# One index copy for a whole ring of gathers, in a graph network of four layers on one NeuronCore

## The chip, the cores and the metric

The kernel runs on one core of a Trainium2 chip. Its engines are TensorE (PE, matrix products), VectorE (DVE), ScalarE (ACT), GpSimd (POOL) and SyncE (SP); each works through its own list of instructions, and they meet only at semaphores. Sixteen DMA engines move data between the device memory and the on-chip memory. The metric is device microseconds of one execution; the time given is the median of several runs. A difference is spoken of as a share of that time.

## What is computed

Four graph layers over 6,250 nodes with 256 features and 100,000 edges, sorted by their target node. Each layer normalises the rows, works on the edges and adds its result to `x`:

```
x = x + L0(h)   # attention: leaky(xl[src] + xr[dst]) -> logits -> softmax over the edges of a node -> weighted sum of xl[src]; then an FFN and two batch norms
x = x + L1(h)   # w = alpha[rel]; sums of w * support[col] at row, and of w * support[row] at col
x = x + L2(h)   # two convolutions: agg[dst] += x[src]; agg @ W_msg + x @ W_self
x = x + L3(h)   # attention with 8 heads: s_u[src] + s_v[dst] -> softmax -> weighted sum of x[src]
```

For this case only one step matters: all four layers need the rows `table[src[e]]` of every edge `e`. That is a gather of 100,352 rows (784 tiles of 128 edges, the last one padded) of 1 KB, and it is made five times: once in L0, once in L1, twice in L2, once in L3.

## The kernel before

**Edges and tiles.** The edge list is cut into `ET = 784` tiles of 128 edges. The source node of each edge lies on chip as a column of integers: `gidx` is 128 x 784, column `t` holding the 128 sources of tile `t`. One indirect DMA, issued by GpSimd, reads one such column and fetches 128 table rows, one to a partition.

**Groups and rings.** The tiles are fetched in groups of `per` tiles. In L0 a group is 4 tiles and the ring of row buffers holds 8 groups; in the three plain passes (L1, L2 twice) it is 4 tiles and 6 groups; in L3 it is 8 tiles and 6 groups. So a pass has 196 groups, or 98 in L3.

**What sets the order.** `gather` (L1001 to L1015) is all that GpSimd does in these passes. For each group it waits until its ring slot is free (L1008, L1009), calls `index_columns` (L996), and issues its indirect DMAs (L1012). `index_columns` copies the group's 4 or 8 index columns out of `gidx`, at an offset that a register holds, to the fixed place `idx[:, b, :]` of slot `b` (L998), waits for that copy on the semaphore `s_own_p` (L999), takes the semaphore back (L1000), and returns the columns. The indirect DMA takes its indices from there. `turns` (L55 to L76) writes the loop: here its body is one turn of the ring, so slot numbers are constants in the code.

**Who frees a slot, who uses it.** SyncE runs `landed_groups` (L965 to L994) beside it. It waits until a group's rows have landed and counts it (`s_landed`, L976, L979), and half a ring later, when the visits that use a group are over, gives its slot back (`ring_free`, L987). In L0 it also writes each group's rows to `edge_rows` in device memory (L1248); in L3 its own loop does that (L1880, L1886 to L1889) and frees the slot when the writes are done and VectorE has read the scores. TensorE multiplies one-hot matrices with the rows (L1103 in the plain passes; L1292, L1304 and L1317 for one visit of L0), and VectorE adds the products to the sums (L956), makes the one-hots (L941) or the features of L0 (L1369, L1376).

**What comes between.** Dense products, softmax passes and a scatter pass lie between the gathers. In the scatter pass (L1722) GpSimd also issues indirect DMAs, each behind a wait and a register operation of its own, without any copy of indices.

Of the kernel before, what the change touches and what calls it, by code (L numbers as in the profile page):

```python
# [5 lines left out]
I32 = mybir.dt.int32  # L6
# [4 lines left out]
P = 128  # L11
# [4 lines left out]
ET = 784  # L16
# [9 lines left out]
GS = 2 * VG  # L26
EG = 4
NEG = ET // EG
RG, RG0 = (6, 8)
# [33 lines left out]
def turns(eng, total, body, lag, steady=None):  # L63
    first = -(-lag // body) * body
    loops = max(0, ((steady or total) - first) // body)
    if loops < 2:
        first, loops = total + lag, 0
    for v in range(first):
        yield Turn(v, v, total, False)
    if loops:  # L70
        with eng.Fori(0, loops) as i:
            for k in range(body):
                yield Turn(i * body + (first + k), first + k, total, True)
        for v in range(first + loops * body, total + lag):
            yield Turn(v, v, total, False)

def build(nc, t, out):
    with ExitStack() as top:
        made = {}

        def own(name):
            made[name] = made.get(name, 0) + 1
            return name if made[name] == 1 else f'{name}_{made[name]}'

        def sb(name, shape, dt=F32, ctx=top):
            return ctx.enter_context(nc.sbuf_tensor(own(name), shape, dt))
# [4 lines left out]
        def sem(name):  # L91
            return top.enter_context(nc.semaphore(name))
# [18 lines left out]
        gidx = sb('gidx', [P, ET], I32)  # L111
# [32 lines left out]
        own_v, own_a, own_p = (sem(f's_own_{k}') for k in 'vap')  # L144
# [801 lines left out]
        def rows_count(name, n=2):  # L946
            return [Count(sem(f's_rows_{name}{b}')) for b in range(n)]
# [45 lines left out]
                sp.wait_ge(ring_free[b], 1)  # L993
                sp.sem_inc(ring_free[b], -1)  # L994

        def index_columns(g, u, ring, per, idx):  # L996
            b = u.c % ring
            g.tensor_copy(idx[:, b, :], gidx[:, bass.ds(u.val * per, per)]).then_inc(own_p, 1)  # L998
            g.wait_ge(own_p, 1)  # L999
            g.sem_inc(own_p, -1)  # L1000
            return [idx[:, b, j:j + 1] for j in range(per)]  # L1001

        def gather(g, table, rows_of, s_rows, ring, per, free, idx):
            top_row = g.to_reg(NP - 1)

            def fetch(u):
                b = u.c % ring
                g.wait_ge(free[b], 1)  # L1008
                g.sem_inc(free[b], -1)  # L1009
                rows = index_columns(g, u, ring, per, idx)  # L1010
                for j in range(per):
                    g.indirect_dma_start(out=rows_of(b * per + j), out_offset=None, in_=table, in_offset=bass.IndirectOffsetOnAxis(ap=rows[j], axis=0), bounds_check=top_row, oob_is_err=True).then_inc(s_rows[b].sem, 16)  # L1012
            for t_ in turns(g, ET // per, ring, 0):
                fetch(t_.at(0))

        def plain_pass(name, table, acc, acc_flat, width, weighted, fold=None, own=None):
            NB = 4
            s_rows = rows_count(name, RG)
            with ExitStack() as ctx:
                G = sb('rows_in', [P, RG * EG, width], F32, ctx)  # L1020
                idx = sb('gather_rows', [P, RG, EG], I32, ctx)
                hot = sb('hot', [P, 2, GS, P], F32, ctx)
                wgt = sb('step_weights', [P, S], F32, ctx) if weighted else None
                ps = [bank(f'ps_p{i}', ctx) for i in range(NB)]
# [196 lines left out]
        def attention_fetch0(LG, attc, room):  # L1221
# [3 lines left out]
            s_rows = rows_count('att0_', RG0)  # L1225
# [2 lines left out]
            row_free = [sem(f's_row_free{b}') for b in (0, 1)]  # L1228
            with ExitStack() as ctx:
                feat = sb('feat', [P, 2, 2 * D], F32, ctx)  # L1230
                idx = sb('gather_rows', [P, RG0, EG], I32, ctx)
                featT = sb('featT', [P, 2, 4, P], F32, ctx)
                psX = [bank(f'psX{b}', ctx) for b in (0, 1)]
                psF = [bank(f'psF{b}', ctx) for b in (0, 1)]
# [620 lines left out]
        def attention_fetch3(LG, SV, rows_room, T_room):  # L1855
            R3 = 6
# [5 lines left out]
            s_rows = rows_count('att3_', R3)  # L1862
# [4 lines left out]
            read3 = [sem(f's_slot_read3{b}') for b in range(R3)]  # L1867
            with ExitStack() as ctx:
                psS = [bank(f'psS{b}', ctx) for b in (0, 1)]
                idx = sb('gather_rows', [P, R3, GS], I32, ctx)  # L1870
                with phase() as block:

                    @block.sync
# [492 lines left out]
```

## Time and profile before

| | |
|---|---|
| Median of 3 runs | 10797.18 us (10796.2 to 10806.08) |
| The profiled execution, its own time | 10752.12 us |
| Its span, first to last instruction | 10750.4 us |
| TensorE busy, mean granted clock | 6331.9 us (59%), 0.739 |
| TensorE weight loads | 4941.0 us (46%) |
| GpSimd busy | 5855.2 us (54%) |
| VectorE busy | 5005.6 us (47%) |
| ScalarE busy | 1331.9 us (12%) |
| DMA, mean over the span | 126 GB/s |

The page cuts the span in 40 slices of 269 us and gives each engine's busy share in tenths. GpSimd's row is `3777740000288888777775777747777167763000`: it has work only in the gathers and the scatter pass, and there it stands at 7 or 8. A busy 7 isn't a free 3: what lies between two instructions of GpSimd has to be looked up in the order of time, and whether it is waiting for someone in the list of waits. The kernel's clock figure is the share of full speed (2.4 GHz) at which TensorE was allowed to run.

### The profile page before, as it was taken

The numbers are of one execution on the slowest core, as the hardware profiler recorded it, in microseconds if no ns is written. First come the engines' busy times: TensorE is split into PE (matmuls) and PEld (weight loads), VectorE is DVE, ScalarE is ACT, GpSimd is POOL, SyncE is SP. The second block draws the span as 40 slices with busy tenths as digits, with TensorE's granted clock in tenths as the row PEclk, the third lists the DMA queues.
The fourth block names the chain that finished last, engine by engine and source line by source line (L and its number), as shares of the span: only waits on it lengthen the run. The fifth ranks groups of instructions, "written<-read, shape, count | busy, mean of one in ns | idle before, by whom it ended". The sixth has DMA issues, their size and how long they took to land. (4 is left out here: it accounts for less than half of the span.)

```text
span 10750.4 us, 137753 instructions
## 1 busy us (share of the span) xinstructions
PE 6331.9 (59%) x24674; PEld 4941.0 (46%) x24675; DVE 5005.6 (47%) x12212; ACT 1331.9 (12%) x3940; POOL 5855.2 (54%) x5805
## 2 busy tenths in 40 slices
PE   4888875757466666555554555555555642222575
PEld 2888864546344444433333444444444442222454
DVE  6555558885444444355553222242222321114888
ACT  2222211213222222100001000010000300000000
POOL 3777740000288888777775777747777167763000
PEclk9898878988777777676766777677777655555798
DMA  4666674541377777644433222222222166663454
GB/s 147 189 190 187 186 231 152 169 136 35 69 104 105 104 104 105 111 134 137 133 117 91 82 82 82 82 75 81 83 83 83 41 193 204 201 193 99 129 170 155
DMA packets 835068, 1358.92 MB, mean 126 GB/s; under 512 B 112279, under 2 KB 488661, under 8 KB 834981
## 3 DMA queue, kind: packets, MB, share of 16 engines
q0 software_dynamic: 315328, 634.04, 26.7%
q1 hardware_dynamic: 385684, 562.46, 16.0%
q10 hardware_dynamic: 133968, 161.50, 4.8%
q8 instruction: 26, 0.43, 0.0%
q14 instruction: 62, 0.50, 0.0%
HBM read 943.05 MB, written 414.50 MB: 126 GB/s over the span
## 5 line engine op out<-in xcount | busy, mean ns | idle before, releaser
L1012 POOL DMA_INDIRECT rows_in<-table,gather_rows x2352 | 2500.5, 1063 | 1034.2 <-issue 511.1
L1103 PE MATMUL ps_p<-rows_in,hot 128*128 x5280 | 2000.5, 542 | 1584.6 <-SPq L976 1328.8
L1103 PEld LDWEIGHTS ps_p<-rows_in,hot 128*128 128x128 f32 x5280 | 1360.3, 271 | 2180.1 <-issue 1928.7
L1722 POOL DMA_INDIRECT scatter_sums<-regionC,idx x880 | 1387.3, 1576 | 307.1 <-issue 246.0
L956 DVE TENSOR_TENSOR regionC<-regionC,ps_p 128x257 f32 (+2 forms) x1320 | 558.6, 423 | 1767.9 <-DVEq L953 1569.1
L1464 PE MATMUL ps_p<-regionA 128*128 128x265 f32 (+1 forms) x3520 | 969.4, 435 | 426.0 <-DVE regionC L956 194.4
L1464 PEld LDWEIGHTS ps_p<-regionA 128*128 128x128 f32 x3520 | 735.3, 214 | 659.8 <-DVE regionC L956 239.3
L1012 POOL DMA_INDIRECT regionB<-table,gather_rows x784 | 848.4, 1082 | 344.5 <-issue 272.2
L1012 POOL DMA_INDIRECT regionC<-table,gather_rows x784 | 817.1, 1042 | 296.7 <-issue 265.1
L1927 PE MATMUL psS<-dst_scores,regionA 128*128 x1760 | 393.4, 362 | 793.7 <-issue 385.4
L1927 PEld LDWEIGHTS psS<-dst_scores,regionA 128*128 128x128 f32 x1760 | 383.7, 330 | 803.4 <-issue 803.4
L1795 PE MATMUL psC<-regionC 128*128 128x128 f32 x1760 | 370.5, 377 | 649.1 <-PEq L1793 647.8
L1807 PE MATMUL psO<-regionA,regionC 128*128 x1760 | 675.1, 552 | 8.8 <-PEq L1806 1.8
L1795 PEld LDWEIGHTS psC<-regionC 128*128 128x128 f32 x1760 | 319.2, 272 | 753.3 <-issue 752.9
L956 DVE TENSOR_TENSOR regionB<-regionB,ps_p 128x265 f32 (+1 forms) x880 | 372.5, 423 | 586.1 <-DVEq L953 472.5
L1537 POOL MEMSET ones<- 128x128 f32 x2 | 0.4, 206 | 1109.1 <-POOLq L2052 940.3
L1807 PEld LDWEIGHTS psO<-regionA,regionC 128*128 128x128 f32 x1760 | 495.1, 295 | 120.7 <-issue 23.8
L1496 DVE TENSOR_TENSOR regionA<-regionA,logits 128x512 f32<-128x512 f32 x880 | 547.6, 684 | 0.0
L1317 PEld LDWEIGHTS psL<-att_cols,featT 128*128 128x128 f32 x3520 | 526.0, 215 | 37.6 <-issue 4.9
L1292 PE MATMUL psX<-regionA,regionB 128*128 x1760 | 528.7, 429 | 21.7 <-PEq L1288 18.6
L1369 DVE TENSOR_TENSOR feat<-regionB,psX 128x512 f32<-128x512 f32 x440 | 301.8, 686 | 499.5 <-DVEq L1368 375.0
L998 POOL COPY gather_rows<-gidx 128x4 int32 (+1 forms) x882 | 221.4, 251 | 468.1 <-POOLq L1009 461.8
(303 smaller groups left out, 8011.7 us busy)
## 6 DMA issues: line engine op xcount, KB each, us to landing
regionA<-edge_rows SPq DMA_DIRECT2D x880, 256.0 KB, 3.2
edge_rows<-regionB SPq DMA_DIRECT2D x196, 512.0 KB
edge_rows<-regionC SPq DMA_DIRECT2D x392, 256.0 KB
regionC<-srcrow_d SPq DMA_DIRECT2D x220, 256.0 KB
scatter_sums<-zero_rows ACTq DMA_DIRECT2D x8, 6400.0 KB, 42.3
regionA<-scatter_sums ACTq DMA_DIRECT2D x49, 1024.0 KB
rows_in<-table,gather_rows POOLq DMA_INDIRECT x2352
regionB<-rrow_d ACTq DMA_DIRECT2D x110, 256.0 KB
```

The lines of the kernel that those rows point to most:

```text
L956: v.tensor_tensor(dst_, dst_, ps[(u.c * VG + j) % nbank][:, 0:width], ALU.add).then_inc(s_add.sem, 1)
L1012: g.indirect_dma_start(out=rows_of(b * per + j), out_offset=None, in_=table, in_offset=bass.IndirectOffsetOnAxis(ap=rows[j], axis=0), boun ...
L1103: x = te.matmul(ps[(u.c * VG + j) % NB][:, 0:width], hot[:, b, 2 * j + k, :], at_tile(G, slot[j] * 2 + k), start=k == 0, stop=k == 1)
L1292: x = te.matmul(psX[b][:, k * D:(k + 1) * D], spread[:, ub, at:at + P], at_tile(A256, nt), start=True, stop=True)
L1317: x = te.matmul(psL[gb][:, col:col + HEADS0], featT[:, b, 2 * k + c, :], attc[:, c, :], start=c == 0, stop=c == 1)
L1369: v.tensor_tensor(feat[:, b, :], G[:, bass.ds(slot * 2, 2), :].rearrange('p a c -> p (a c)'), psX[b][:, :], ALU.add).then_inc(own_v, 1)
L1464: x = te.matmul(ps[(u.c * VG + j) % NB][:, 0:width], hot[:, b, 2 * j + k, :], Gs[:, b * GS + 2 * j + k, :], start=k == 0, stop=k == 1)
L1496: v.tensor_tensor(o, i, w, ALU.mult).then_inc(aux_full[b], 1)
L1722: g.indirect_dma_start(out=scat, out_offset=bass.IndirectOffsetOnAxis(ap=idx[:, b, j:j + 1], axis=0), in_=sums[:, b, j, :], in_offset=None ...
L1795: x = te.matmul(psC[b][:, j * P:(j + 1) * P], hot[:, b * Q + j, :], same[:, b * Q + j, :], start=True, stop=True)
L1807: x = te.matmul(psO[2 * b + j // 2][:, j % 2 * D:(j % 2 + 1) * D], pairs[:, b * Q + j, :], at_tile(SUP, nt[j // 2]), start=True, stop=True)
L1927: x = te.matmul(psS[b][:, j * HEADS3:(j + 1) * HEADS3], spread[:, b, j * P:(j + 1) * P], at_tile(SV, nt[j // 2]), start=True, stop=True)
```

## The change

Before, GpSimd copies the indices of one group at a time, 4 or 8 columns, with a wait for the copy in each group. After, it copies the indices of a whole turn of the ring at once (24, 32 or 48 columns), to one of two buffers in turn, at the head of each turn, and ahead of the wait for the ring's first slot. The DMAs take their index columns from that buffer. The loop's body is two turns of the ring instead of one, so that the buffer's number is a constant in the code. `idx` is twice as large. Nothing else changes.

```
-        def index_columns(g, u, ring, per, idx):
-            b = u.c % ring
-            g.tensor_copy(idx[:, b, :], gidx[:, bass.ds(u.val * per, per)]).then_inc(own_p, 1)
-            g.wait_ge(own_p, 1)
-            g.sem_inc(own_p, -1)
-            return [idx[:, b, j:j + 1] for j in range(per)]
-
         def gather(g, table, rows_of, s_rows, ring, per, free, idx):
             top_row = g.to_reg(NP - 1)
+            groups = ET // per
+
+            def indices(u):
+                n = ring if not isinstance(u.val, int) else min(ring, groups - u.val)
+                g.tensor_copy(idx[:, u.c // ring % 2, 0:n * per], gidx[:, bass.ds(u.val * per, n * per)]).then_inc(own_p, 1)
+                g.wait_ge(own_p, 1)
+                g.sem_inc(own_p, -1)
 
             def fetch(u):
                 b = u.c % ring
+                if b == 0:
+                    indices(u)
                 g.wait_ge(free[b], 1)
                 g.sem_inc(free[b], -1)
-                rows = index_columns(g, u, ring, per, idx)
                 for j in range(per):
-                    g.indirect_dma_start(out=rows_of(b * per + j), out_offset=None, in_=table, in_offset=bass.IndirectOffsetOnAxis(ap=rows[j], axis=0), bounds_check=top_row, oob_is_err=True).then_inc(s_rows[b].sem, 16)
-            for t_ in turns(g, ET // per, ring, 0):
+                    at = b * per + j
+                    g.indirect_dma_start(out=rows_of(at), out_offset=None, in_=table, in_offset=bass.IndirectOffsetOnAxis(ap=idx[:, u.c // ring % 2, at:at + 1], axis=0), bounds_check=top_row, oob_is_err=True).then_inc(s_rows[b].sem, 16)
+            for t_ in turns(g, groups, 2 * ring, 0):
                 fetch(t_.at(0))
...
-                idx = sb('gather_rows', [P, RG, EG], I32, ctx)
+                idx = sb('gather_rows', [P, 2, RG * EG], I32, ctx)
```

The two other allocations of `idx`, in L0 and L3, change in the same way.

GpSimd's list at the head of the gather loop of L0, before. `gather_rows` is `idx`, `regionB` holds the ring of row buffers:

```order
L998 ISA [waits s_ring_free0]
L998 COPY gather_rows<-gidx 128x4
L1012 DMA regionB<-table,gather_rows 128x256 [waits s_own_p]
L1012 DMA regionB<-table,gather_rows 128x256 x3
L998 ISA [waits s_ring_free1]
L998 COPY gather_rows<-gidx 128x4
L1012 DMA regionB<-table,gather_rows 128x256 [waits s_own_p]
L1012 DMA regionB<-table,gather_rows 128x256 x3
```

The same place, after:

```order
L71 ISA
L1002 COPY gather_rows<-gidx 128x32
L1014 DMA regionB<-table,gather_rows 128x256 [waits s_own_p,s_ring_free0]
L1014 DMA regionB<-table,gather_rows 128x256 x3
L1014 DMA regionB<-table,gather_rows 128x256 [waits s_ring_free1]
L1014 DMA regionB<-table,gather_rows 128x256 x3
```

The wait for the slot has moved from the copy to the group's first DMA, and the copy and its own wait are gone from every group but the first of a turn.

The head of the gather loop of L3, after; its ring slots are freed by `s_slot_free30` to `s_slot_free35`, and `regionC` holds its rows:

```order
L1002 COPY gather_rows<-gidx 128x48
L1014 DMA regionC<-table,gather_rows 128x264 [waits s_own_p,s_slot_free30]
L1014 DMA regionC<-table,gather_rows 128x264 x7
L1014 DMA regionC<-table,gather_rows 128x264 [waits s_slot_free31]
L1014 DMA regionC<-table,gather_rows 128x264 x7
```

Here 48 DMAs follow one copy, where one copy stood ahead of each 8.

## Rows read from the trace of the kernel before

**Rows 1.** Busy time by stage: the five gathers, all engines.

```profile
core 0: us, PE busy (x) PEld busy (x) DVE busy (x) ACT busy (x) POOL busy (x), PEclk, DMA share, GB/s
260.50:1510.50 1250.00, 1116.77 (x6995) 1029.50 (x6996) 676.12 (x1094) 259.63 (x437) 904.26 (x980) 0.88 0.61 187
4530.50:5719.50 1189.00, 676.21 (x1752) 463.28 (x1752) 626.38 (x1416) 0.00 (x0) 842.68 (x980) 0.69 0.43 130
5782.40:7029.40 1247.00, 736.56 (x2046) 518.00 (x2046) 343.68 (x598) 38.64 (x97) 900.86 (x980) 0.72 0.28 82
7142.50:8388.90 1246.40, 729.99 (x2046) 520.03 (x2046) 341.84 (x598) 38.62 (x97) 900.85 (x980) 0.73 0.28 82
8611.90:9792.40 1180.50, 392.19 (x1755) 382.51 (x1756) 207.57 (x733) 0.00 (x0) 838.13 (x882) 0.50 0.68 200
```

**Rows 2.** Waits of GpSimd in the third gather, then in the fifth: total, times, longest.

```profile
POOL gather_rows L998 <- POOLq L1009: 63.0, 1, 63.0
...
POOL gather_rows L998 <- POOLq L1009: 266.9, 9, 223.1
```

**Rows 3.** GpSimd in order of time, third gather: start, length, instruction, idle before it.

```profile
6302.58 1.01 POOL L1012 DMA_INDIRECT rows_in<-table,gather_rows  x1 [0.30 <-issue]
6303.90 1.01 POOL L1012 DMA_INDIRECT rows_in<-table,gather_rows  x1 [0.30 <-issue]
6304.91 0.20 POOL L998 COPY gather_rows<-gidx 128x4 int32 x1
6305.90 1.04 POOL L1012 DMA_INDIRECT rows_in<-table,gather_rows  x1 [0.79 <-POOLq L1000]
...
6310.91 0.19 POOL L998 COPY gather_rows<-gidx 128x4 int32 x1
6311.89 1.67 POOL L1012 DMA_INDIRECT rows_in<-table,gather_rows  x1 [0.79 <-POOL gather_rows L998]
```

**Rows 4.** GpSimd in order of time, scatter pass.

```profile
3211.29 1.56 POOL L1722 DMA_INDIRECT scatter_sums<-regionC,idx  x1 [0.30 <-issue]
3213.16 1.56 POOL L1722 DMA_INDIRECT scatter_sums<-regionC,idx  x1 [0.30 <-POOLq L1716]
```

**Rows 5.** Line L998, all copies: duration in ns, least, median, most.

```profile
L998 POOL COPY gather_rows<-gidx x882: 185/193/1268, 260.6 to 9780.9; 128x4 int32 x153, 128x8 int32 x19, 128x4 int32<-128x4 int32 x4, 128x8 int32<-128x8 int32 x1
```

**Rows 6.** Copies of L998 alone by stage: length, GpSimd busy (count), clock, DMA.

```profile
260.50:1510.50 1250.00, 56.00 (x196) 0.88 0.61 187
4530.50:5719.50 1189.00, 40.60 (x196) 0.69 0.43 130
5782.40:7029.40 1247.00, 50.69 (x196) 0.72 0.28 82
7142.50:8388.90 1246.40, 52.94 (x196) 0.73 0.28 82
8611.90:9792.40 1180.50, 21.14 (x98) 0.50 0.68 200
```

**Rows 7.** VectorE in order of time, beside the last row of Rows 3.

```profile
6311.43 1.22 DVE L941 TENSOR_TENSOR hot<-iota,rel 128x1024 f32<-128x1024 f32 x1
```

**Rows 8.** A wide GpSimd instruction, from the groups of instructions.

```profile
L257 POOL IOTA regionA<- 128x392 f32 x1 | 0.5, 453 | 0.0
```

**Rows 9.** TensorE in order of time, first gather: starts of four visits' transposes.

```profile
1001.27 0.75 PE L1304 MATMUL psF<-ident,feat 128*128 128x128 f32 x4 [1.85 <-PEq L1302]
...
1005.51 1.09 PE L1304 MATMUL psF<-ident,feat 128*128 128x128 f32 x4
...
1009.09 0.63 PE L1304 MATMUL psF<-ident,feat 128*128 128x128 f32 x4
...
1011.24 0.64 PE L1304 MATMUL psF<-ident,feat 128*128 128x128 f32 x4
```

**Rows 10.** GpSimd in order of time, a longer pause of the third gather.

```profile
6269.72 1.01 POOL L1012 DMA_INDIRECT rows_in<-table,gather_rows  x1 [1.76 <-issue]
```

**Rows 11.** DMA queues during the third gather, the code's own queue.

```profile
q14 instruction: 3, 0.02, 0.0%
```

More of the change, by code:

```diff
@@ L1230, in attention_fetch0 @@
                 feat = sb('feat', [P, 2, 2 * D], F32, ctx)
-                idx = sb('gather_rows', [P, RG0, EG], I32, ctx)
+                idx = sb('gather_rows', [P, 2, RG0 * EG], I32, ctx)
                 featT = sb('featT', [P, 2, 4, P], F32, ctx)
@@ L1869, in attention_fetch3 @@
                 psS = [bank(f'psS{b}', ctx) for b in (0, 1)]
-                idx = sb('gather_rows', [P, R3, GS], I32, ctx)
+                idx = sb('gather_rows', [P, 2, R3 * GS], I32, ctx)
                 with phase() as block:
```

## The prediction, made before the changed kernel was run

> **What bounds the kernel now.** The page's busy shares name no engine: TensorE 59%, GpSimd 54%, VectorE 47%. So I read the kernel by stage, taking the five stretches from a gather's first index copy to its last DMA [rows 1]. They add up to 6112.9 us of the span of 10750.4. GpSimd is busy for 71 to 72% of each. TensorE is at 54 to 59% in the three plain passes, at 33% in the fifth stretch, and at 89% in the first. VectorE is between 18 and 54%. No engine is full, so I looked at whom GpSimd waits for. In the third gather its only wait for a ring slot is the one ahead of the first group (63.0 us, once) [rows 2]; the first, second and fourth gathers show the same, one wait at the start. From then on a slot was always free: the consumers are ahead, and GpSimd never stops. Only the fifth gather has more, nine waits with 266.9 us, 223.1 of them ahead of the first group; some 44 us in eight waits lie inside it [rows 2].
>
> What GpSimd does in that time stands in its own order of time [rows 3]. Within a group, one indirect DMA follows the other at 1.32 us (6302.58, 6303.90): 1.01 us of work and 0.30 us of idle. Where a group ends, the index copy starts at once (6304.91 = 6303.90 + 1.01) and takes 0.20 us, but the next DMA starts only 0.79 us after its end. From one group's first DMA to the next one's is 5.99 us (6305.90 to 6311.89). Four DMAs at 1.32 would be 5.28. The copy therefore costs 0.71 us of a period of 5.99, of which its own busy time is only 0.2: the rest is the wait for its semaphore. This is what bounds the five gathers: GpSimd's chain of issue, copy included.
>
> **What the change removes.** Copies before: 196 in each of four gathers and 98 in the fifth, 882 in all [rows 5, 6]. After, one to a turn of the ring: 196/8 gives 25 in the first, 196/6 gives 33 in each plain pass, 98/6 gives 17 in the fifth, so 25 + 99 + 17 = 141. Removed: 171 in the first gather, 163 in each plain pass, 81 in the fifth, 741 together. At 0.71 us each: 121 + 3 x 116 + 57 = 526 us.
>
> **What is left at a group's boundary.** The wait for the slot and the taking back of its semaphore stay, and now stand directly ahead of a DMA instead of ahead of a copy. Does the gap there fall to the 0.30 us that lies between DMAs, or stay at 0.79? Two places speak to it. The copy starts with no gap after the fourth DMA [rows 3], although the slot's wait, its semaphore and a register operation stand between them: they ran while the DMA did. And in the scatter pass each DMA has a wait and a register operation of its own, some of them two waits, and the gap is still 0.30 us, also where the trace names the semaphore line L1716 as what ended it [rows 4]. So I take 0.30. The other end is 0.79, by which a removed copy brings only its own 0.2 us: 741 x 0.2 = 148 us.
>
> **What is added.** The 141 copies left are wider, 24 to 48 columns instead of 4 or 8. No row shows that width. The nearest are a copy of 4 columns at 0.193 us [rows 5] and a generated tile of 392 columns at 0.453 us [rows 8]. By the first the width costs nothing, by the second 0.26 us each, 37 us in all. Since 48 columns are nearer to 4 than to 392, I take 0.05 each: 7 us. The first copy of each gather now runs ahead of the wait for the first slot, which is 63.0 us long in the third gather [rows 2], so that one is hidden: 5 x 1 us at most, left in the bounds. The loops turn half as often, 68 times instead of 136; their branch is hidden in the zero gap ahead of a copy [rows 3], and it still stands ahead of one.
>
> **What contention does.** The copies' mean is more than 0.193 us: 56.00/196 = 0.29 in the first gather, 0.21 in the second, 0.26 and 0.27 in the next two, 0.22 in the fifth [rows 6]. With these means a removed copy is worth 0.78, 0.70, 0.75, 0.76 and 0.71 us, and the sum is 549 us. But the order of time shows what the excess is [rows 3, 7]: the DMA that starts at 6311.89 takes 1.67 us, 0.66 more than its neighbours, while VectorE's one-hot instruction of 1.22 us had begun at 6311.43 and ended at 6312.65. GpSimd's next instruction stands still until VectorE's is over, whichever it is. The number of such VectorE instructions doesn't change, so most of the delay moves from the copies to DMAs. Of the 23 us between the two sums I keep 10.
>
> The Trainium skill states this as a lock ("SBUF — State Buffer", section "Who interferes with whom"): a VectorE instruction with two inputs in SBUF blocks a GpSimd instruction that reads SBUF until it has finished, and the one that issued second waits. The rows just read agree in kind [rows 3, 7]. The same section infers that descriptor generation isn't touched by such a VectorE instruction; here an indirect DMA was, and the row decides. By that inference the delay would have belonged to the copies alone, and the sum would be the 549 us.
>
> **The fifth gather** won't give all of its 57 us. Of its waits for slots inside the stretch, some 44 us, a part is set by others: the rows must land, be written out again and be read. With GpSimd sooner at the slot, each such wait grows by what it gained since the last one. Eight waits in 98 groups leave most of the gain; I take off 12 us (the ends: 0, and all 57). What it competes for is the DMA engines, 0.68 busy at 200 GB/s [rows 1].
>
> **Sum.** 526 - 7 + 10 - 12 = 517 us. The profiled execution took 10752.12 us, so 10235 for the changed kernel on the same terms; the span hides nothing, as launch and end are within 2 us of it. The runs' median is 45 us above the profiled execution, 10797.18, and what is asked for is a median: 10797 - 517 = 10280 us, 4.8% less.
>
> **Rivals.**
>
> *A, the boundary gap stays.* The 0.79 us isn't the copy's but belongs to a group's start, and only 0.2 us a copy goes: 10797 - 148 = 10649. For it: the first DMA of a group is 1.04 us long against 1.01 [rows 3], so something does differ there. Against it: the scatter pass [rows 4]. Chance 0.06.
>
> *B, TensorE becomes the bound of the first gather.* There it is busy for 1116.77 of 1250 us [rows 1]. If that work couldn't shrink, then with the same slack of 7% for its pauses the stage would stop at 1200 us: 50 instead of 121 us gained, and if the fifth gather gives nothing either, another 45 lost: 10280 + 71 + 45 = 10396; with the first alone 10351. Against it: one visit takes 4.24 us in one place (1001.27 to 1005.51) and 2.15 us in another (1009.09 to 1011.24) [rows 9], and the stage's granted clock is 0.88, a mean of stretches at full clock (2.4 GHz) and at half. 441 visits at 2.15 us are 948 us; the gather would take 1250 - 121 = 1129. The pace asked of TensorE goes from 2.83 to 2.56 us a visit, which it keeps at 2.4 GHz and not at 1.2. The half-speed stretches are short beside a ring of 8 groups, 42 us of work, which evens them out. Chance 0.10.
>
> *C, the end on the other side: loading code.* The loop body of a gather is twice as long, 96 DMAs in the fifth gather instead of 48, with waits beside them. If the branch back no longer found its target at hand, each of the 68 turns would wait for code. The price of a turn is unknown; the longest pause ahead of a DMA that no one is named for is 1.76 us, 1.46 over the usual [rows 10], which would give 68 x 1.46 = 99 us, so 10379. It decides the sign from 517/68 = 7.6 us a turn, and at 10 us a turn the kernel would be at 10797 - 517 + 680 = 10960. Against it: the code's queue moved 3 packets in the whole third gather [rows 11], with the loops of all engines running, so loops of the present sizes load nothing. Chance 0.03 for the small price and 0.02 for one that makes the kernel slower.
>
> The Trainium skill has the rule behind this ("Runtime: NRT & Kernel Launch", section "Instruction fetch mechanics"): a taken branch whose target isn't in the two pages held forces a fetch, and a page is 256 instructions. By it the longest new body, some 130 instructions by the list, still stays inside, and rival C would cost nothing. No row here shows a loop that leaves the window.
>
> **How the numbers follow.** The forecast has 0.79, A 0.06, B 0.10, C 0.05. The forecast's own bounds: all of the copies' excess gone, no wider copies, the fifth gather in full, the five first copies hidden, gives 549 + 5 = 554, so 10243; runs differ by some 10 us and the median may sit 0.3% off the profile's offset, so 10210 at the low end. At the high end, 37 us for wide copies, no credit for contention and nothing from the fifth gather: 526 - 37 - 57 = 432, so 10365. To take in most of B and the small price of C the range goes to 10400: 10210 to 10400 leaves out A, the dear C and the edges, less than 2 in 10. Faster by more than 0.2% (22 us, about what a measurement of this kernel can tell from no change): everything but the dear C and an unforeseen nothing, 0.96. Within 0.2%: 0.02. Slower: 0.02.
>
> **What the new profile would show.** Copies: 141 instead of 882. In GpSimd's order of time, the gap between the last DMA of a group and the first of the next is 0.30 us; 0.79 us there means A. The five stretches: about 1130, 1075, 1130, 1130 and 1135 us. GpSimd's busy share in them rises to some 76%, since idle goes rather than work. Waits for ring slots inside the first four gathers stay near nothing; if the first shows many, it is B. Pauses of over 1 us at every turn of the loop mean C. If GpSimd's gaps close as told and the stretches still don't shrink, the reading that GpSimd sets their length is wrong, and with it the whole forecast.

## The result, and the profile after

The changed kernel took 10956.85 us (median of 4 runs, 10934.54 to 10962.57), beside 10799.43 us for the kernel before: the ratio is 1.0141, with a 95% interval of 1.0124 to 1.0159. It is slower; the forecast was 10280. The profiled execution took 10954.17 us, against 10752.12.

First what the profile after says of GpSimd. The copies of the new line, then the third gather at a turn of the ring, in order of time (start, length, instruction, idle before it):

```profile
L1002 POOL COPY gather_rows<-gidx x141: 202/214/1254, 255.3 to 9955.2; 128x24 int32 x96, 128x32 int32 x24, 128x48 int32 x16, 128x16 int32<-128x16 int32 x5
```

```profile
6575.67 1.01 POOL L1014 DMA_INDIRECT rows_in<-table,gather_rows  x1 [0.30 <-issue]
6576.69 0.21 POOL L1002 COPY gather_rows<-gidx 128x24 int32 x1
6577.79 1.05 POOL L1014 DMA_INDIRECT rows_in<-table,gather_rows  x1 [0.89 <-issue]
6579.14 1.01 POOL L1014 DMA_INDIRECT rows_in<-table,gather_rows  x1 [0.30 <-POOLq L1011]
```

There are 141 copies, as worked out, each 0.02 us longer than a narrow one (214 ns against 193 in [rows 5]). The thirteen DMAs ahead of this copy, over the ends of three groups, all follow each other at 0.30 us where no group finds its slot taken: GpSimd's part went as told. But the stages, which answer to [rows 1], did not all follow:

```profile
255.30:1706.10 1450.80, 1179.11 (x6760) 1066.73 (x6761) 657.77 (x1062) 250.21 (x422) 839.94 (x809) 0.80 0.51 160
4740.70:5975.80 1235.10, 614.80 (x1752) 433.75 (x1752) 637.04 (x1413) 0.00 (x0) 807.40 (x817) 0.67 0.42 125
6035.50:7211.20 1175.70, 670.44 (x2032) 476.62 (x2033) 336.50 (x590) 38.91 (x98) 855.75 (x817) 0.71 0.30 88
7321.50:8497.60 1176.10, 663.16 (x2034) 474.44 (x2034) 335.68 (x590) 38.84 (x98) 847.15 (x817) 0.69 0.30 88
8722.00:9977.20 1255.20, 382.52 (x1712) 373.02 (x1712) 204.24 (x712) 0.00 (x0) 812.98 (x801) 0.50 0.63 187
```

The first gather went from 1250 to 1451 us, the second from 1189 to 1235, the fifth from 1180 to 1255; the two of layer 2 fell from 1247 to 1176. Together that is +180 us; the other 22 of the 202 lie between the stages. What lengthens them stands in the waits of the first gather, kernel after, then before (who waited, for whom, total us, times, longest):

```profile
ACT featT L1275 <- ACTq L1274: 998.5, 326, 20.6
DVE feat L1371 <- DVEq L1370: 522.0, 239, 21.0
POOL regionB L1014 <- POOLq L1011: 373.6, 101, 10.4
```

```profile
ACT featT L1273 <- ACTq L1272: 689.9, 307, 5.3
DVE feat L1369 <- DVEq L1368: 345.3, 222, 3.6
```

GpSimd, which had waited for no slot here, now does: 373.6 us in 101 gaps put down to line L1011, the wait for the slot. In 12 of them only the usual 0.30 or 0.89 us passed; the other 89 hold 366 us. ScalarE's longest wait for TensorE's transposes grew from 5.3 to 20.6 us. The start of the gather shows how. First TensorE and ScalarE, then GpSimd, all in the kernel after (start, length, instruction, idle before it):

```profile
276.53 0.63 PE L1306 MATMUL psF<-ident,feat 128*128 128x128 f32 x4
279.01 0.63 PE L1306 MATMUL psF<-ident,feat 128*128 128x128 f32 x4
284.18 0.60 ACT L1275 ACTIVATE featT<-psF 128x512 f32<-128x512 f32 x1 [9.24 <-ACTq L1274]
288.21 1.08 PE L1306 MATMUL psF<-ident,feat 128*128 128x128 f32 x4 [1.88 <-issue]
302.66 0.60 ACT L1275 ACTIVATE featT<-psF 128x512 f32<-128x512 f32 x1 [17.88 <-ACTq L1274]
303.40 1.84 PE L1319 MATMUL psL<-att_cols,featT 128*128 128x4 f32 x8 [12.39 <-PEq L1312]
```

```profile
301.62 1.01 POOL L1014 DMA_INDIRECT regionB<-table,gather_rows  x1 [0.30 <-issue]
302.94 1.01 POOL L1014 DMA_INDIRECT regionB<-table,gather_rows  x1 [0.30 <-issue]
303.95 0.22 POOL L1002 COPY gather_rows<-gidx 128x32 int32 x1
305.06 1.04 POOL L1014 DMA_INDIRECT regionB<-table,gather_rows  x1 [0.89 <-issue]
```

TensorE writes the transposes of one visit and the next to two buffers in turn, each with a semaphore of its own, and can't begin those of the visit after next before ScalarE has copied the first. So a copy belongs to the last transposes of its own buffer: the one at 284.18 to those of 276.53, the one at 302.66 to those of 279.01. These were over at 279.64, and ScalarE, which in between made one copy and issued one DMA, began their copy 23.0 us later. TensorE's next products stood for 12.39 us behind that. From 279 to 303 GpSimd issued a DMA every 1.32 us. The transposes of 288.21 were copied at 323.8.

I measured the lateness of all 440 copies of the first gather: from the end of the copy's own transposes, or of ScalarE's copy before where that is later, to the copy's start. It is 0.13 us where nothing holds it. Over 3 us late were 5 in the kernel before (3.8 us at most) and 67 in the kernel after (20.6 at most); over 5 us none and 34.

Is it TensorE's signal that is late, or the engine that waits for it? The trace also keeps the times at which each semaphore changed, though not all of them where copies are late. For the copy at 302.66 the semaphore was raised at 302.54, not at 279.64. Where both changes of a copy's semaphore are on record, the raising came over 1 us after the end of TensorE's transposes in 131 of 332 cases (34.4 us at most) in the kernel after, and in 65 of 271 (2.8 at most) in the kernel before. Where it is on record, the semaphores that ScalarE and VectorE raise for TensorE in the same gather were never raised over 0.2 us after the end of the instruction, in either kernel. So it is TensorE's signals that come late. They do so while GpSimd's indirect DMAs run: between the first gather and the next indirect DMAs, 1376 us, the kernel after has all 787 such waits for TensorE on record, none with a late signal. No other engine's DMAs are needed for it: in its third gather GpSimd's queue moves all but 0.06 of the 101.58 MB, and at least 93 of 373 such signals on record are over 1 us late.

### The profile page after: what moved, and what is told of

It reads as the page before. It is cut to its first block and busy times, and to the rows that moved or that the text cites. A ratio compares the mean times of both kernels' runs of the same rounds, so it can differ in the third digit from the quotient of the medians.

```text
span 10952.4 us, 135271 instructions
## 1 busy us (share of the span) xinstructions
PE 6223.2 (57%) x24674; PEld 4885.9 (45%) x24675; DVE 5015.1 (46%) x12212; ACT 1331.5 (12%) x3940; POOL 5628.6 (51%) x5064
## 5 line engine op out<-in xcount | busy, mean ns | idle before, releaser
L1105 PE MATMUL ps_p<-rows_in,hot 128*128 x5280 | 1831.2, 506 | 1654.4 <-issue 527.8
L1105 PEld LDWEIGHTS ps_p<-rows_in,hot 128*128 128x128 f32 x5280 | 1269.1, 253 | 2176.6 <-issue 1965.2
L1319 PEld LDWEIGHTS psL<-att_cols,featT 128*128 128x128 f32 x3520 | 557.6, 228 | 218.8 <-issue 185.5
L1319 PE MATMUL psL<-att_cols,featT 128*128 128x4 f32 x3520 | 509.8, 268 | 155.3 <-ACT featT L1275 67.4
L1294 PE MATMUL psX<-regionA,regionB 128*128 x1760 | 562.5, 451 | 19.7 <-PEq L1290 17.9
```

Source lines behind the costliest of these rows:

```text
L1105: x = te.matmul(ps[(u.c * VG + j) % NB][:, 0:width], hot[:, b, 2 * j + k, :], at_tile(G, slot[j] * 2 + k), start=k == 0, stop=k == 1)
L1294: x = te.matmul(psX[b][:, k * D:(k + 1) * D], spread[:, ub, at:at + P], at_tile(A256, nt), start=True, stop=True)
L1319: x = te.matmul(psL[gb][:, col:col + HEADS0], featT[:, b, 2 * k + c, :], attc[:, c, :], start=c == 0, stop=c == 1)
```

## The experiments

All kernels here share one edit: loaded register values that an engine waits against (the visits counted by SyncE, the groups of TensorE and VectorE) first go through a maximum with zero into registers of their own.

```
+            for r, h in zip(regs, held):
+                eng.reg_alu(h, r, 0, ALU.max)
```

The runs were made in six sets, each on one chip and with the kernel before beside them; a kernel has 2 to 9 runs in a set. The kernel before didn't take the same time in all of them, and this turned out to be what decides the sign:

| set, chip | before | what ran, median us (ratio, interval) |
|---|---|---|
| 1, no. 11 | 10797 | before with the edit 10802; after 10982 (1.017, 1.015 to 1.019); pause 10782 (0.998, 0.997 to 0.999); mixed 10692 (0.991, 0.989 to 0.992) |
| 2, no. 7 | 10705 | brief 10130 (0.946, 0.945 to 0.948); long 10333 (0.965, 0.963 to 0.967); two 10367 (0.969, 0.967 to 0.971); order 10436 (0.975, 0.973 to 0.976) |
| 3, no. 15 | 10710 | after 10128 (0.946, 0.944 to 0.947); brief 10128 (0.946, 0.944 to 0.948) |
| 4, no. 7 | 10762 | brief 10849 (1.009, 1.006 to 1.013); long 10597 (0.985, 0.982 to 0.987); order 10605 (0.985, 0.982 to 0.988) |
| 5, no. 4 | 10724 | two 10372 (0.967, 0.965 to 0.970); after 10139 (0.946, 0.943 to 0.948); mid 10211 (0.952, 0.950 to 0.955) |
| 6, no. 11 | 10772 | two 10640 (0.988, 0.985 to 0.991); mid 10777 (1.000, 0.998 to 1.002) |

I call sets 2, 3 and 5 (before at 10705 to 10724) the prompt condition and 1, 4, 6 and the result itself (10762 to 10799) the late one.

**The edit, and the kernel after with it.**

> The kernel before, with one edit that all the kernels of this study share: each number loaded from memory that a semaphore is waited against is first passed through max(value, 0), one register operation each. It is the yardstick for the others. Every theory expects 10,800 us, within 0.3%, and the five gathers at 1250, 1189, 1247, 1246 and 1180 us.

> The changed kernel with the same shared edit. Every theory expects 10,957 us, within 0.3%, and the five gathers at 1451, 1235, 1176, 1176 and 1255 us.

Measured 10802 and 10982: the edit costs nothing before, and the kernel after stays 1.7% slower.

**Pause: a tiny instruction with its wait at each group that has no copy.** After's wide copies, loop and buffers stay; only GpSimd's halt of the kernel before comes back.

```
                 if b == 0:
                     indices(u)
+                else:
+                    g.memset(pause_tile[:, :], 0.0).then_inc(own_p, 1)
+                    g.wait_ge(own_p, 1)
+                    g.sem_inc(own_p, -1)
```

> The changed kernel (one index copy to a turn of the ring), but at each other group GpSimd clears one word per partition and waits for that on its own semaphore, as it waited for the group's copy before. Theory P (what the removed copies gave was a moment in which GpSimd's queue runs dry, in which the signals of TensorE get through to ScalarE and VectorE): back to the time before, 10,780 us, between 10,740 and 10,840, with the five gathers within 1% of 1250, 1189, 1247, 1246, 1180, and the waits for ring slots gone. Theory W (the wide index buffer, or the doubled loop body, slows the gathers or loads code): the pauses only add to it, 10,957 + 741 x 0.5 = 11,300 us at most and not under 10,950. Theory C (TensorE is the bound of the first gather at its granted clock): also not under 10,950, since the pause gives TensorE nothing.

Measured 10782. Adding 741 instructions with their waits to the kernel after makes it 200 us faster: its first gather fell from 1424 to 1237 us. So not the width of the copies, the loop's length or TensorE's capacity cost the time, but the missing halt. The fifth gather took 1236 us, not within 1% of 1180; in the kernel before of this set it took 1221.

**Mixed: ring-wide copies in layer 2 alone.**

```
-                if b == 0:
+                if b % every == 0:
                     indices(u)
...
+                        gather(g, table, lambda k: G[:, k, 0:D], s_rows, RG, EG, ring_free, idx, every=1 if weighted else RG)
+                        gather(g, T0, lambda k: G[:, k, :], s_rows, RG0, EG, ring_free, idx, every=1)
+                        gather(g, T4, lambda k: G[:, k, :], s_rows, R3, GS, free3, idx, every=1)
```

`indices` copies `every` groups at a time.

> One index copy to a turn of the ring in the two passes of L2 alone, where neither SyncE nor ScalarE issues DMAs; one to a group everywhere else, from the doubled buffer and with the doubled loop body. Theory P: the two passes keep their gain of 71 and 70 us, the three others are back at the lengths before: 10,799 - 141 = 10,658 us, between 10,630 and 10,700. Theory W: the first, second and fifth gathers stay as slow as in the changed kernel as far as the buffer or the body does it: 10,900 us or more. Theory C says the same as P here.

Measured 10692, 0.9% ahead of before, at the upper part of the range: layer 2's passes took 1176 and 1181 us, and the first two gathers 1276 and 1212, some 25 more than before. Their copy stood ahead of the slot's wait, with 0.89 us behind it instead of 0.79.

**Brief and long: an instruction between the groups that nobody waits for.** Does GpSimd have to halt, or only to leave the DMAs for a while? In L0, L1 and L3 (layer 2 as in the kernel after):

```
+                elif filler is not None:
+                    g.wait_ge(filled, 1)
+                    g.sem_inc(filled, -1)
+                    g.memset(filler[:, :], 0.0).then_inc(filled, 1)
```

The wait is for the memset of the group before, which is long over; `filler` has 1 column (brief), 640 (long) or, later, 256 (mid).

> The kernel after, and in the gathers of att0, l1 and att3 a memset of one column (some 0.1 us by the rows of such memsets) at each group that copies no indices; GpSimd doesn't wait for it (its semaphore is taken back a group later), so the queue behind it isn't held up. The two passes of layer 2 are as in the kernel after. Stages of the shared-edit kernel after: 1424, 1235, 1186, 1177, 1265 us, total 10982. Theory D (the signals of TensorE get through only where GpSimd waits for a semaphore of its own): nothing gets better, 10970 to 11010, first stage 1410 to 1450. Theory T (they need some time, about 0.7 us, without an indirect DMA at work, waiting or not): too brief to help, 10940 to 11010. Theory N (any instruction between two groups' DMAs that is no DMA lets them through): the three stages lose their waits for ring slots, first stage 1150 to 1200, total 10600 to 10720.

> As the kernel with the brief memset, but 640 columns wide: by the rows of 1 and 128 columns (0.10 and 0.206 us) about 0.63 us, so that groups follow each other at the pace of the kernel before, without a wait. Layer 2 as in the kernel after. Theory D (only a wait for a semaphore of its own helps): TensorE's signals stay late, the first stage stays at 1400 us or above, total 10950 to 11200. Theory T (time without a DMA is what helps): the three stages come back to those of before, 1247, 1189 and 1221 us, total 10982 - 177 - 46 - 44 = 10715, 10680 to 10760. Theory N gives the same as T here.

**Two, and order: how often a copy, and on which side of the slot's wait.** Two is mixed with

```
-ring_free, idx, every=1 if weighted else RG)
+ring_free, idx, every=2 if weighted else 3)
-                        gather(g, T0, lambda k: G[:, k, :], s_rows, RG0, EG, ring_free, idx, every=1)
+                        gather(g, T0, lambda k: G[:, k, :], s_rows, RG0, EG, ring_free, idx, every=2)
```

and order is mixed with

```
-                if b % every == 0:
-                    indices(u)
                 g.wait_ge(free[b], 1)
                 g.sem_inc(free[b], -1)
+                if b % every == 0:
+                    indices(u)
```

> Index copies (with their wait) at every second group in att0 and l1, every third in the passes of layer 2, every group in att3: how many pauses are needed? The kernel with one at each group except in layer 2 (one in six) took 10692: stages 1276, 1212, 1176, 1181, 1208. If the harm grows with the stretch between pauses (P): att0 and l1 lie between that and the kernel after (1424 and 1235), nearer to the good end since a pause of 0.9 us every 8 DMAs still lets the signals through: att0 1230 to 1350, l1 1190 to 1225; layer 2 loses 33 x 0.8 = 26 us of copies and wins back part of the some 45 us of waits, 1150 to 1190 each. Total 10620 to 10770, most likely 10690. If one pause in two groups were as bad as one in eight, att0 alone would be at 1400 and the total at 10830.

> As the kernel with ring-wide copies in layer 2 alone (10692), but the index copy stands behind the wait for its slot again, as in the kernel before. There the gap from copy to DMA was 0.80 us, with the copy ahead of the slot's wait it was 0.89 to 0.92. If that order is all that made att0 1276 instead of 1250 and l1 1212 instead of 1189: 47 us less in these two, some 10 in att3, a few in layer 2: 10620 to 10650. If the two differ for another reason (the double buffer, the loop of twice the length): 10680 to 10700.

Brief took 10130, which no theory here had allowed (N, the nearest, said 10600 to 10720), long 10333, two 10367 and order 10436. The contradiction stood in the stages that the edit hadn't touched: layer 2, code that had taken 1186 and 1177 us in set 1, now took 1112 and 1116. Two readings were left, the chip or the brief memset, and the kernel after itself could tell them apart.

> The kernel after with the shared edit once more, beside the brief memset on one chip. In the last four runs the passes of layer 2 took 1109 to 1120 us with the very code that had taken 1176 to 1186 in the four before, and the kernel before itself took 10705 instead of 10797: the two sets ran on different chips. Theory H (the delay that eats the gain is a property of the chip and not of the code): on the chip of the last set this kernel takes 10100 to 10180, about as the kernel with the brief memset, and on the chip of the first set 10960 to 11000. Theory N (an instruction between the groups that is no DMA lets the signals through): it takes 10900 to 11000 on either, and the brief memset beside it 10130.

> The kernel with the brief memset once more. Theory H: within 60 us of the kernel after on the same chip, whichever chip it is. Theory N: 10100 to 10200 on any chip, some 800 us below the kernel after.

After took 10128 and brief 10128: the memset does nothing in this condition, and the change is worth 5.4%. Theory H holds against N, but only in part, as set 4 showed. The kernel after in set 3, by stage:

```profile
255.90:1366.50 1110.60, 1030.01 (x6973) 962.02 (x6973) 675.40 (x1094) 260.87 (x436) 849.68 (x809) 0.93 0.69 210
4378.50:5452.00 1073.50, 639.72 (x1752) 443.18 (x1752) 625.07 (x1416) 0.00 (x0) 809.30 (x817) 0.74 0.48 144
5511.80:6630.10 1118.30, 694.11 (x2046) 496.75 (x2046) 342.71 (x598) 38.82 (x98) 856.90 (x817) 0.74 0.32 92
6739.70:7856.50 1116.80, 696.23 (x2046) 499.61 (x2046) 341.66 (x597) 38.87 (x98) 855.07 (x817) 0.75 0.32 92
8079.70:9175.90 1096.20, 393.38 (x1760) 383.59 (x1760) 205.38 (x745) 0.00 (x0) 824.97 (x801) 0.50 0.73 216
```

and its waits in the first gather, to be held against those of the result:

```profile
ACT featT L1283 <- ACTq L1282: 808.0, 424, 5.0
DVE feat L1381 <- DVEq L1380: 315.4, 282, 3.5
POOL regionB L1021 <- issue: 208.9, 677, 1.6
...
POOL regionB L1021 <- POOLq L1018: 36.6, 74, 0.9
```

None of ScalarE's 440 copies was over 3 us late (2.3 at most), and in each of them the semaphore was raised within 0.02 us of the end of the transposes. GpSimd waited for no slot: the 36.6 us are its usual gaps of 0.30 and, behind a copy, 0.89. The 28 us between 274.34 and 302.66, in which the kernel of the result made one copy, had ten here (start, length, instruction, idle before it; set 3, ScalarE, a part):

```profile
297.43 0.60 ACT L1283 ACTIVATE featT<-psF 128x512 f32<-128x512 f32 x1 [2.47 <-ACTq L1282]
299.58 0.60 ACT L1283 ACTIVATE featT<-psF 128x512 f32<-128x512 f32 x1 [1.55 <-ACTq L1282]
301.73 0.60 ACT L1283 ACTIVATE featT<-psF 128x512 f32<-128x512 f32 x1 [1.55 <-ACTq L1282]
```

**The same three kernels again, for the late condition.**

> The kernel with the brief memset, once more, for a chip on which the kernel before takes about 10797 (the kernel after was at 10982 there, its first stage at 1424 us). If the kernel before takes 10797 here: theory D or T (only a wait, or only some time without a DMA, lets TensorE's signals through) gives 10960 to 11010 and a first stage of 1400 to 1450; theory N (any instruction between groups does) 10600 to 10750. If the kernel before takes 10707: 10130, as twice before.

> The kernel with the memset of 640 columns, for the same chip. Where the kernel before takes 10797: theory D (a wait is needed) 10950 to 11200 with a first stage above 1400; theory T (time without a DMA is enough) 10680 to 10760 with a first stage of 1200 to 1260. Where it takes 10707: 10333, as before.

> Index copies at each group as in the kernel before, with its order, and ring-wide ones in layer 2 alone. Where the kernel before takes 10797: the first two stages as in it (1247 and 1189), layer 2 as in the kernel with the same copies there (1176 and 1181), the last 1208: 10640, 10600 to 10670. Where it takes 10707: 10436.

Set 4 ran on chip 7, the chip of set 2, and was late. So it isn't a property of a chip but a condition that one can be in, for a whole set at least. No total lies in the range of a theory: brief's 10849 is between that of N and that of D and T, long's 10597 below T's 10680 to 10760, with the kernel before 35 us lower than those ranges took it. What decides is the first gather. Brief has 1396 us and 322 us of waits for slots: any instruction between the groups isn't enough (N falls). Long has 1234, without any wait for itself: a halt isn't needed (D falls); what helps is time without an indirect DMA (T). The kernel after wasn't run in this set, so whether brief helps a little isn't shown. Stage length, GpSimd's busy time, clock and DMA of the first gather, brief, then long:

```profile
255.70:1652.00 1396.30, 863.59 (x980) 0.81 0.53 166
```

```profile
256.10:1490.50 1234.40, 963.37 (x980) 0.89 0.61 188
```

and GpSimd's waits for slots there, brief, then long:

```profile
POOL regionB L1028 <- POOLq L1025: 322.1, 107, 8.3
```

```profile
POOL regionB L1028 <- POOLq L1025: 58.0, 49, 5.7
```

GpSimd does 100 us more work in the long one and is through 162 us sooner. Order took 10605 (10640 expected): with the copy behind the slot's wait the first two gathers are at 1245 and 1188 us, so the order accounts for mixed's 25 us in each (0.10 us at each of 196 copies is 20 of them).

**How long, and how often.**

> Index copies with their wait at every second group in att0 and l1, every third in layer 2, every group in att3 (10367 where the kernel before takes 10705). Where the kernel before takes 10760 to 10800 this asks how often GpSimd must leave the indirect DMAs: if one pause of some 0.9 us every 8 DMAs is enough, att0 and l1 are at 1180 to 1250 and 1132 to 1170, the total at 10480 to 10600, ahead of all so far there; if it must be every 4 DMAs, att0 is at 1330 or more and the total at 10700 to 10850.

> The kernel after, as the anchor of this chip and this hour. 10128 where the kernel before takes about 10707, 10850 to 10990 where it takes 10760 to 10800. The same chip (number 7) has shown both 10705 and 10762 for the kernel before, so this decides which condition the two others are to be read by.

> The memset without a wait, 256 columns wide: some 0.30 us, between the brief one (0.12 us) and the long one (0.65 us), the gap behind it 0.16 to 0.19 us as there. Where the kernel before takes about 10707: 10130 + (0.3 - 0.12)/(0.65 - 0.12) x 203 = 10200. Where it takes 10760 to 10800: if the time without a DMA is what counts, between the brief (10849, first stage 1396) and the long one (10597, 1234): 10650 to 10800; if there is a least length, one of the two ends.

> Index copies at every second group in att0 and l1, every third in layer 2, every group in att3, for the condition in which the kernel before takes 10760 to 10800, which the last call did not meet. There: 10480 to 10600 if a pause every 8 DMAs is enough in att0 and l1, 10700 to 10850 if it must be every 4. Where the kernel before takes about 10710: 10370, as twice before.

> The memset of 256 columns without a wait, for the same condition: 10650 to 10800 if the time without a DMA counts in proportion, 10850 (as the brief one) or 10600 (as the long one) if there is a least length. Where the kernel before takes about 10710: 10211, as before.

Set 5 was prompt and gave the interpolated numbers (mid 10211 for 10200; after 10139). Set 6 was late. In it mid took 10777, between brief and long: no least length shows. Its first gather with those of the other kernels, late condition, and what each has at a group's end over the 0.30 us between DMAs:

| kernel | extra time off the DMAs | first gather, late | prompt | copies over 5 us late of 440, late condition | latest copy, us |
|---|---|---|---|---|---|
| after | 0 | 1424, 1451 | 1111, 1108 | 29, 34 | 22.7, 20.6 |
| brief | 0.0 us | 1396 | 1108, 1109 | 32 | 15.6 |
| mid | 0.2 us (0.33 of memset, 0.16 of gap) | 1365 | 1148 | 22 | 12.9 |
| two | 0.8 us at each second group | 1347 | 1180, 1188 | 23 | 8.0 |
| long | 0.5 us (0.65 of memset, 0.16 of gap) | 1234 | 1198 | 0 | 4.6 |
| pause | 0.7 us at each group | 1237 | - | 1 | 5.3 |
| order | 0.7 us at each group | 1245 | 1250 | 0 | 3.7 |
| before | 0.7 us at each group | 1247, 1250 | - | 1, 0 | 5.4, 3.8 |

It is the long delays that go. Copies over 3 us late are as many in long (71) as in brief (70) or after (67, 64), but at half a microsecond off the DMAs in each group none is over 5 us late, and the stage is 162 to 217 us shorter. In the prompt condition no copy is over 3.5 us late in any of these kernels. That signals get through in the breaks shows in the kernel before as well: 92 of its copies in the first gather are over 1.5 us late, and 38 of them got their signal between the last DMA of a group and the first of the next, though these breaks are 18% of the time. The others got theirs while the DMAs went on.

In the prompt condition the stage follows the sum of GpSimd's own times, in the late one it runs against it. Two (10640) lies between its two expectations, 10600 and 10700: a pause in every second group isn't enough in the first gather, but in the second (1157 against 1132 prompt) and in layer 2 (1154, with a copy at each third group) it gives back most.

No version is best in both conditions: after is in the prompt one (10128, 10139), long in the late one (10597), and there order is level with it. Long, order and two beat the kernel before in both, long by 3.5% and 1.5%, order by 2.5% and 1.5%, two by 3.1% and 1.2%.

## Why the prediction was wrong

**The size of GpSimd's part: right in the main.** 741 copies fell away, the gap at a boundary is 0.30 us (rival A falls), wide copies cost 0.02 us where 0.05 was taken. In the prompt condition, where nothing else moves, the stages are 1111, 1074, 1118, 1117 and 1096 us, for 1130, 1075, 1130, 1130 and 1135 foretold, and the kernel gains 582 us (10710 - 10128) for 517.

**Two terms too small.** One wasn't in the sum. The pause of 1.76 us of [rows 10] isn't a single one: the kernel before has 38 like it in its five gathers, one in 80 to 96 DMAs, 49 us over the usual gaps. In set 3 five are left, 6 us: 43 us gained. Kernels in which GpSimd waits for itself at each group have them (pause all 38), brief and long have five; why, no run shows. The other is contention. I let most of the copies' delay by VectorE move to the DMAs. It didn't: in the first gather the DMAs' excess over 1.015 us sums to 53 us before and 48 in set 3. With the copies' whole excess and the pauses the sum is 526 + 23 + 43, less 3 for the width and 14 for the 0.89 us behind a wide copy, 575 of the 582. In that the inference of the Trainium skill that the prediction weighed ("SBUF — State Buffer", "Who interferes with whom"), by which the delay belonged to the copies alone, gives the better sum. For single DMAs it doesn't hold: all 75 DMAs of over 1.1 us in the third gather before stand beside a one-hot instruction like the one of [rows 7], of the other 709 only 58 do.

Two readings were off, without weight for the sum: TensorE is at 57 to 59% in the plain passes, not 54 [rows 1], and the first gather has 440 visits, not 441.

**The step that failed: "From then on a slot was always free: the consumers are ahead, and GpSimd never stops."** It was read off a kernel with a pause in each group, and taken as holding without it: "Waits for ring slots inside the first four gathers stay near nothing", and the sum has no term for them. In the late condition they don't. There the gaps put down to slots in the first gather are 374 us, against 37 in the prompt run of the same code, and of the 340 us by which that gather is longer they are 337. The other gathers are 162, 57, 59 and 159 us longer, 777 together. From the prompt condition to the late one the kernel after loses 829 us (10128 to 10957) and the kernel before 90 (10710 to 10799). The gain of 582 was made and more than given back: 739 less 582 is the 157 us of the result. What holds the slots is TensorE's signals reaching ScalarE and VectorE late, which then stand for up to 21 us, while GpSimd issues its indirect DMAs one behind the other. That the missing pause is the cause is shown by pause against after in set 1 and by long and order against brief in set 4; the path on which the signals are held is not.

The trace of the kernel before could have warned me. 136 of ScalarE's 440 copies were 1 to 4 us late in it, although the engine was idle. In the order kernel of set 2, with the same pauses, 79 were, and there every signal whose times are on record was prompt, so that much is ScalarE's own; the rest was TensorE's signals, late already with the pauses in place. The visit of 4.24 us [rows 9] wasn't such a sign: its four products at 1002.08 took 2.07 us, against 1.03 at 1009.56, at a granted clock of 0.55 from 1001 to 1008 and 1.00 from 1009 to 1013: that is the clock, as I had read it.

**Rival B** (TensorE becomes the bound of the first gather) had the right sign of symptom, slot waits in the first gather, and the wrong cause: with TensorE at 1030 us of work in 1111 at a clock of 0.93 it kept up where its signals came in time. The lower clock after (0.80 against 0.88) goes with its idle time. **Rival C** (loading code) falls: in set 3, over the second, third and fourth gather, no gap between two DMAs is over 0.32 us, turns of the loop included; the two long ones of the first gather and the three of the fifth add 6 us.

**The chances.** 0.96 for faster left no place for a mechanism that the profile didn't name. The prediction did say what would show it wrong: gaps that close and stretches that don't shrink. In three of the five that is what the result shows.

**What stays open.** What puts a chip into the late condition, and by which path GpSimd's DMAs then hold TensorE's signals. It isn't the chip (number 7 was found in both) and it isn't code. Between the gathers little differs: in order, from the end of the first gather to the start of the second 3019 us in set 2 and 3020 in set 4; in the kernel after 3012 and 3015 prompt, 3035 and 3051 late, where more visits are left when the last DMA is issued. No run here put work on other cores of the chip, so that they are the cause wasn't tried. Nor did a run spread the extra time evenly over the DMAs: whether breaks are needed, or only a slower mean pace of the DMAs, isn't shown.

## What to carry to other kernels

A short halt in one engine can be what lets the others' signals through: before taking it out, look whether waits between two other engines end late while it works, and bound the case in which they do. A queue of indirect DMAs from GpSimd, issued without a break, did this here; half a microsecond of other work in each group of four left no copy over 5 us late. And measure such a change on more than one chip and hour, with the kernel before beside it: the same code was 1.7% slower and 5.4% faster.

## What the runs showed of the hardware

- An indirect DMA of 128 rows held GpSimd for 1.01 us (the median; 1.01 to 1.03 in the gathers looked at) and the next followed 0.30 us later, with or without a slot's wait and its semaphore between them; the pace of 1.32 us held for a whole ring. Beside VectorE's one-hot instruction single ones took up to 2.06 us.
- Behind a copy with a wait for its own semaphore the next DMA came after 0.79 us, and after 0.89 if a slot's wait stood behind the copy as well. Without a wait it came 0.16 us (long memset) or 0.19 us (brief) after the end.
- With GpSimd's DMAs back to back, in the late condition, TensorE raised the semaphore of a finished result up to 34.4 us after its end, and ScalarE stood idle for up to 22.7 us behind such a signal (set 1); semaphores raised by ScalarE and VectorE were on time. In the prompt condition TensorE's were too, with the same code.
- All of ScalarE's 440 copies of the first gather are on record in every trace. Changes of semaphores aren't: of the 880 of these copies the late traces have 616 to 739, the prompt ones 871 to 880, and outside the gathers the late ones have nearly all. So each trace here tells by itself in which condition it was taken.
